# Residual and output bias of the last mixture folded into TensorE's PSUM accumulation

## The reference, cut to what matters

```
x = x + gnn0(layernorm(x), adj, ...)       # 4 heads, 2048 x 2048 mask
x = x + ffn0(layernorm(x), ...)            # 8 experts, top 2
x = x + gnn1(layernorm(x), adj, ...)       # one averaged attention
x = x + ffn1(layernorm(x), route_id, ...)  # the change touches this one
```

```
h = relu(flat @ Wi.T + bi)                          # 128 -> 256
for l in range(2):
    h = relu(h + shared_l(h) + routed_l(h))         # one expert per group of 32 rows
out = h @ Wo.T + bo                                 # 256 -> 128
x + out is returned
```

## Time and profile before

| what | value |
|---|---|
| time, median of 3 runs | 739.09 us (736.9 to 740.69) |
| the profiled execution's own time | 739.58 us |
| its span, first to last instruction | 737.8 us |
| PE busy, share of the span | 617.6 us, 84% |
| DVE busy | 526.4 us, 71% |
| ACT busy | 388.4 us, 53% |
| POOL busy | 164.8 us, 22% |
| chain that ended last | PE 65%, DVE 18%, ACT 7%, issue 5%, POOL 3%, DMA 1% |
| POOL L483, the adds of ysb to x | 16 instructions, 42.2 us, mean 2641 ns |
| ACT L1063, the evictions to ysb | 16 instructions of 277 to 278 ns |

### The profile page before, as it was taken

One profiled execution on the slowest core, in us unless ns is written; L12 is line 12 of the kernel. 1 busy time (PEld: TensorE's weight loads), 2 busy tenths in 40 slices (PEclk: granted clock), 3 DMA queues, 4 the chain that ended last, 5 costly groups with the idle time before them and its releaser, 6 DMA issues.

```text
span 737.8 us, 14828 instructions
## 1 busy us (share of the span) xinstructions
PE 617.6 (84%) x5288; PEld 467.8 (63%) x5288; DVE 526.4 (71%) x1071; ACT 388.4 (53%) x761; POOL 164.8 (22%) x130
## 2 busy tenths in 40 slices
PE   2856776999999999899999979984589889889696
PEld 1645664867868678677887636763547647647453
DVE  6699989677677776678663579269597998997300
ACT  1767895777867678567887455431022222222231
POOL 4201032011111111102111113416403603602100
PEclk9977995999999999999999989996769979969888
DMA  7446630011110111101111011010546716716643
GB/s 156 84 79 115 172 58 1 2 59 58 59 58 1 59 58 59 59 2 59 58 59 58 0 58 56 2 45 3 150 136 189 226 58 197 217 57 200 213 130 113
DMA packets 30702, 63.08 MB, mean 86 GB/s; under 512 B 4556, under 2 KB 7636, under 8 KB 30644
## 3 DMA queue, kind: packets, MB, share of 16 engines
q1 hardware_dynamic: 27156, 52.50, 23.5%
q0 software_dynamic: 2624, 9.44, 6.6%
q10 hardware_dynamic: 864, 0.33, 0.2%
HBM read 69.59 MB, written 1.05 MB: 96 GB/s over the span
## 4 chain that ended last, share of the span: by engine, by line
PE 65%; DVE 18%; ACT 7%; issue 5%; POOL 3%; DMA 1%; SPq 1%; DVEq 0%; ACTq 0%
PE bank L598 16%; PE bank L610 12%; PE bank L558 10%; PE bank L679 6%; PE bank L543 5%; PE bank L716 4%; PE bank L709 3%; ACT arena L956 2%; POOL reg_b L455 2%; DVE reg_c L1355 2%; DVE arena L1210 2%; PE bank L534 2%; DVE arena L1198 2%; ACT ysb L913 1%; PE bank L507 1%
## 5 line engine op out<-in xcount | busy, mean ns | idle before, releaser
L956 ACT ACTIVATE arena<-sbc,nd 128x512 bf16<-128x512 f32 x204 | 130.2, 718 | 33.5 <-PE bank L558 33.5
L448 POOL TENSOR_TENSOR x<-x,ysb 128x512 f32<-128x512 f32 x36 | 61.9, 1720 | 304.9 <-ACT ysb L913 300.6
L610 PEld LDWEIGHTS bank<-arena,reg_c 128*128 128x128 f32 x1024 | 116.8, 192 | 7.2 <-issue 7.2
L598 PE MATMUL bank<-hTc,arena 128*128 128x512 f32 x256 | 120.9, 628 | 0.0
L610 PE MATMUL bank<-arena,reg_c 128*128 128x128 f32 x1024 | 116.9, 275 | 0.0
L558 PE MATMUL bank<-reg_b,arena 128*128 128x99 bf16 x2048 | 102.4, 213 | 11.3 <-DVE arena L1210 11.2
L558 PEld LDWEIGHTS bank<-reg_b,arena 128*128 128x128 bf16 x2048 | 100.6, 101 | 14.1 <-issue 12.1
L903 ACT ACTIVATE reg_c<-bank,b 128x512 f32<-128x512 f32 x128 | 87.9, 688 | 36.3 <-PE bank L598 36.3
L1355 DVE SCALAR_TENSOR_TENSOR reg_c<-reg_b,nd,reg_c 128x512 f32<-128x512 f32 x144 | 96.3, 740 | 0.0
L1198 DVE TENSOR_TENSOR arena<-maskT,arena 128x2048 bf16<-128x2048 bf16 x48 | 60.8, 1266 | 49.8 <-ACT arena L956 49.6
L598 PEld LDWEIGHTS bank<-hTc,arena 128*128 128x128 f32 x256 | 51.1, 202 | 64.6 <-issue 64.6
(11 more groups left out here) (164 smaller groups left out, 729.1 us busy)
## 6 DMA issues: line engine op xcount, KB each, us to landing
arena<-in_wrT SPq DMA_DIRECT2D x128, 256.0 KB, 3.0
reg_c<-in_adj POOLq DMA_DIRECT2D x16, 512.0 KB, 5.9
arena<-in_w1T SPq DMA_DIRECT2D x16, 512.0 KB, 3.9
arena<-in_w2T SPq DMA_DIRECT2D x16, 512.0 KB, 4.8
x<-in_x SPq DMA_DIRECT2D x4, 256.0 KB, 4.6
out_x<-x POOLq DMA_DIRECT2D x4, 256.0 KB, 3.8
arena<-in_wsT SPq DMA_DIRECT2D x1, 512.0 KB, 3.7
arena<-in_gW ACTq DMA_DIRECT2D x2, 64.0 KB, 4.0
```

Source lines behind the costliest of these rows:

```text
L448: nc.gpsimd.tensor_tensor(xi, xi, ysb[:, e % 3, :].rearrange("p (t d) -> p t d", d=P), ALU.add).then_inc(s_acc, 1)
L598: mm(bank[b][:, :], w1[:, s, e % 2, c * P:(c + 1) * P], hTc[:, :], start=True, stop=True).then_inc(full[b], 1)
L610: last = mm(bank[b][:, i * P:(i + 1) * P], hid[:, e % 2, c, i * P:(i + 1) * P], w2[:, s, e % 2, c, :], start=(c == 0), stop=(c == HC - 1))
L956: last = af(ind[:, q, 1, j, :], sbc[:, h, :], ACT.Relu, bias=nd[:, q * QT + j, h:h + 1], scale=BIG)
```

## The change

POOL's bias add (L477) and its four adds a chunk (L483) are gone; POOL waits for the four evictions and stores. On PE `output` first multiplies the identity with the row tile of x, as moving operand, and a row of ones with the bias row `bo`, into the same 128 columns of PSUM, and then adds the two products as before. ACT copies the bank straight into x and no longer waits for a slot of `ysb`. Since x is addressed by the loop variable, `output` takes the chunk as a second argument.

```
@@ gpsimd
-                pool.wait_ge(s_xn, 3 * C + c + 1)
-                xi = x[:, c * CT:(c + 1) * CT, :]
-                nc.gpsimd.tensor_tensor(xi, xi, bo.unsqueeze(1).to_broadcast([P, CT, P]),
-                                        ALU.add).then_inc(s_xb, 1)
-                pool.wait_ge(s_xb, C + c + 1)
-                for i in range(CT):
-                    pool.wait_ge(ev["y"], FFN_Y + c * CT + i + 1)
-                    xi = x[:, c * CT + i, :]
-                    nc.gpsimd.tensor_tensor(xi, xi, ysb[:, 0, i * P:(i + 1) * P], ALU.add).then_inc(s_acc, 1)
-                pool.wait_ge(s_acc, FFN_Y + c * CT + CT)
+                pool.wait_ge(ev["y"], FFN_Y + c * CT + CT)
                 pool.dma_start(outv[:, c * CT:(c + 1) * CT, :],
                                x[:, c * CT:(c + 1) * CT, :]).then_inc(s_out, 16)
@@ tensor
-            def output(i):
+            def output(i, c):
                 r, b = i % 2, 3 + i % 2 * 2
                 ready(b - 1)
                 use(b, "y")
+                mm(bank[b][:, 0:P], ident[:, :], x[:, bass.ds(c * CT + i, 1), :].rearrange("p o d -> p (o d)"),
+                   start=True, stop=False)
+                mm(bank[b][:, 0:P], ones[0:1, :], bo[0:1, :], start=False, stop=False)
                 for kc in range(KC):
                     last = mm(bank[b][:, 0:P], htt[:, r, L, kc * P:(kc + 1) * P], woT[:, kc, :],
-                              start=(kc == 0), stop=(kc == KC - 1))
+                              start=False, stop=(kc == KC - 1))
                 last.then_inc(full[b], 1)
@@ scalar
-            def output(i):
+            def output(i, c):
                 b = 3 + i % 2 * 2
-                y_slot(CT)
+                k.event("y")
                 got(b)
-                af(ysb[:, 0, i * P:(i + 1) * P], bank[b][:, 0:P], ACT.Copy).then_inc(ev["y"], 1)
+                af(x[:, bass.ds(c * CT + i, 1), :].rearrange("p o d -> p (o d)"), bank[b][:, 0:P],
+                   ACT.Copy).then_inc(ev["y"], 1)
```

More of the change, by code:

```diff
@@ L773, in _, with chunk1 @@
             pe.wait_ge(s_wc, 1 + L * KC)
-            def chunk1(next_rows):
+            def chunk1(c, next_rows):
                 for t in range(QT):
@@ L794, in chunk1 @@
                         hidden(i + 1)
-                    output(i)
-            chunk1(2)
+                    output(i, c)
+            chunk1(0, 2)
             per = {"att": 2, "prob": 16, "rows": 4, "xn": 1, "hTc": 1, "ohx": 1, "htt": 20, "y": 4}
@@ L801, in _ @@
                 k.enter(c, 2, per)
-                chunk1((c + 1) % C)
+                chunk1(c - 1, (c + 1) % C)
                 k.leave(C - 2, per)
@@ L817, in _ @@
                 for j in pair:
-                    output(j)
+                    output(j, C - 1)
         @block.scalar
@@ L1081, in _ @@
                         hidden(i + 1)
-                    output(i)
+                    output(i, c - 1)
                 k.leave(C - 1, per)
```

## The result

| | kernel before | changed kernel |
|---|---|---|
| time, median of 20 runs each | 737.91 us (736.48 to 740.69) | 741.74 us (737.33 to 746.46) |
| ratio of the times | 1 | 1.0047, 95% interval 1.0028 to 1.0066 |
| profiled execution's own time, span | 739.58, 737.8 us | 742.76, 741.0 us |
| PE busy | 617.6 us x5288 | 623.0 us x5352 |
| POOL busy | 164.8 us | 117.2 us |

The ratio compares the means of the 20 runs: 3.5 us more, 0.47% of 738. Between the medians it is 3.8 us. Its interval leaves out 1, so the change is slower beyond the scatter of the runs, if only by a little. The forecast was +2.3 us against 739.09 us, the median of the three runs known then. The time, 741.7 us, lies within the range and 0.3 us from the forecast 741.4; that it is so close is in part luck, since those three runs lay 1.2 us above the median of 20.

A forecast was written before the change was run, and what follows sets the result against it. PE was taken to bound the dense stretches, DVE the pass starts. Added matmuls 4.11, address set up 0.48, bias add -2.49 and tail 0.2 summed to +2.3 us on 739.09: 741.4 us, range 737.8 to 744.3.

The forecast's parts named there:

- three signs of being wrong: Added instructions clearly above 0.457 us, first four L1355 staying at 3.56 us, or another clock course at the borders.
- The price of the added matmuls: PE, each output: four added instructions at 0.114 us, 0.457 us; three outputs a pass on the path, 4.11 us.
- Nothing is idle between: PE around one output: no idle time from ACT's last hidden tile to the following layer, so longer output moves everything.
- The address set up: PE behind the wait in loop passes: 0.08 us each, six on the path, +0.48 us.
- The fourth output and the border: End of a pass: PE's 2.97 us idle before xn covers this output's 0.46 us; uncovered, 1.4 us more in all.
- POOL's waiting adds cost DVE nothing: POOL's 128x128 adds: removing them frees 42.2 us of POOL time, and DVE gains nothing.
- The bias add: Start of each mixed pass: without POOL's 128x512 add, PE's wait ends 0.83 us earlier, 2.49 us over three.
- The rival that half of the gain is lost at the clock: Behind PE's wait: the 0.83 us won are spent at 1.2 GHz; sum +3.5 us, 742.6 us; chance 0.17.
- the clock stays up or rises earlier: Pass borders: more PE work, less idle time; saves up to 5.9 us in full, 735.5 us; chance 0.12.
- The tail: Last chunk: 0.91 us PE work, 0.15 hidden, 0.56 gained from POOL's add; +0.2 us, between 0.0 and 0.5.
- The slow rivals: Borders: POOL's store and cast hit layer norm harder, or bias add gives DVE no gain; each 743.9 us, chance 0.08.
- the clock rival: Pass borders: clock staying up or rising earlier, 1.96 us a pass; in two passes of three, the range's low end.

The follow-up runs named there:

- bias128: Changed kernel with the bias product taking the identity and 128 equal rows of bo, not one row; 736.53 us, ratio 0.9973 to the kernel before.
- the hoisted form: As bias128, with residual and bias products ahead of the wait for ACT's last hidden tile; 732.32 us, ratio 0.9904 to the kernel before.
- the second pair of executions: Kernel before and changed kernel, both unchanged, profiled once more; wait's end to first turn summed to 20.51 us and 18.33 us.
- 64 rows: Changed kernel with 64 rows of ones and of bo in place of one; one execution, 1.38 us from output to next layer.
- the constant address: Changed kernel with the residual reading row tile i of chunk 0 in every chunk; one execution, dense stretches 33.64, 33.64, 33.65 us.

## Why the prediction came out right, point by point

**What bounds.** Right. PE pays in the dense stretches, DVE at a pass's start: each removed or added piece came out where the windows had put it. The prediction named three signs of being wrong, and two of them are in the trace: the added instructions took clearly more than 0.457 us, and the clock at the borders took another course. The total is right, the sum behind it only in part.

**The price of the added matmuls.** Mis-sized. The forecast took 4 x 0.114 = 0.457 us from a run of equal shapes; measured are 0.83 us an output. The step that failed was to charge the one-row product by L574 beside L573: their durations (272 and 277 ns) are equal, but a duration does not contain the distance to the neighbour. The starts of the two would have warned of it in the trace of before. These lines are from the routing products of the last chunk of the first mixture, where 128 rows and one row alternate:

```profile
404.40 0.39 PE L573 MATMUL bank<-wgT,hTc 128*128 128x8 f32 x2
404.72 0.38 PE L574 MATMUL bank<-bg,ones 1*128 1x8 f32 x2
405.03 1.60 PE L598 MATMUL bank<-hTc,arena 128*128 128x512 f32 x2
```

The starts are 0.32 and 0.31 us apart at the full clock although the products have only 8 columns; in bias128 a product of 128 columns between others of 128 rows came in 0.22 us.

**What of it lay on the path.** Part of the dear price was covered by a wait I had overlooked. The dense stretch of the first pass grew by 2.09 us, 0.70 us an output and not 0.83. These are ACT and PE of the kernel before behind the output of the earlier trace rows:

```profile
564.81 0.63 ACT L1045 ACTIVATE sbc<-bank,arena 128x128 f32<-128x128 f32 x2
565.49 1.13 PE L709 MATMUL bank<-arena,sbc 128*128 128x256 f32 x4
566.56 1.09 PE L716 MATMUL bank<-arena,sbc 128*32 128x256 f32 x16
```

L709 starts just when ACT's next tile is written, 0.14 us behind L706, and L716 comes 1.07 us later. In the changed kernel ACT is done long before, L700 follows L697 in 0.11 us, and L707 follows at 555.22, 0.96 us later. That gives 0.03 + 0.11 = 0.14 us back (0.14 - 0.11 and 1.07 - 0.96), and 0.83 - 0.14 = 0.69 us are left. "Nothing is idle between" was thus wrong in the small: right behind `output` PE had a second wait, with the dearer restart that follows one. This is also why the hoisted form cost less than I expected: there PE goes from the start of `hidden` to L700 in 1.45 us, before in 1.32 us, and gets 0.11 us back behind it.

**The address set up.** Right in kind, 0.10 us each instead of 0.08 us.

**The fourth output and the border.** Right: +0.03 us over three borders, the cover of 2.97 us held. The store did not come earlier against the layer norm, as I had it: at the second border it starts 1.25 us after the first step, before 0.82 us. Two steps are stretched there as before.

**POOL's waiting adds cost DVE nothing.** Right; the twelve tiles take 8.03 us with and without them.

**The bias add.** Right to 0.01 us for the wait itself, 2.50 against 2.49 us, and right that DVE does not stand for the whole of POOL's 1.52 us: the one stretched instruction loses 0.84 us, and 0.44 us of POOL's 1.52 are its own loss (1.08 us alone).

**The clock.** The rival that half of the gain is lost at the clock had its sign wrong. That it gives +3.5 us, what was measured, is chance. From the wait's end to the first turn PE needed 1.6 us less over three passes, 2.2 us less in the second pair of executions, and 1.2 us less in the kernel without the add. In eleven profiled executions of kernels without the add at that place the sum was 15.96 to 21.38 us, ten of them below 19.6; with it twice 20.5. The granted clock of the changed kernel reached 1.00 at about 544 us, 11.5 us after the transposes; in the kernel before at about 549 us, 15 us after them. The prediction had "the clock stays up or rises earlier" as another rival, for another reason (more work for PE), with 5.9 us in full; something of this kind happened, to 1.6 us.

How far it belongs to the change shows in the runs. The granted clock of the whole program was 0.909 on the mean in the 23 runs of the kernel before, 0.913 in the 12 without the add, and 0.919 in the 20 of the changed kernel. From the first transposes on it was 0.87 in both traces of the kernel before and 0.90 to 0.93 in the eleven others. The clock also goes with the spread of the changed kernel's own runs: its fastest, 737.33 us, had 0.932, its slowest, 746.46 us, 0.916. That kernels without the add at the border run at the higher clock is thus shown; what makes it rise is not. In the trace with 64 rows, PE's first wait ended as early as in the changed kernel and the clock still rose 14.8 us after the transposes.

**The tail.** Mis-sized: +1.70 us in place of +0.2 us. 0.92 us of it is the last two outputs up to the store. The forecast had 0.91 - 0.15 us for PE there and -0.56 us for POOL; measured are +1.45 and -0.53 us, so it is the price of the products again. 0.27 us is the way up to the first turn (9.39 us after the transposes, before 9.12), over a stretch that was 8.4 to 9.8 us in all the traces. The other 0.51 us lie between the first turn and the end of PE's wait for the last expert weights (15.21 us, before 14.70). That the first two outputs vanish in this wait was right: up to the next turn, which follows it, the kernels with 64 rows and with the constant address, which have all the added products, need 15.64 and 15.56 us, the kernel before 15.68 and 15.49 us. Why the changed kernel needs 16.19 and 16.14 us stays open.

**The slow rivals** did not happen: the layer norm's border stayed the same, and DVE's gain was real. The low end of the range is worked out wrongly: two passes of three at the clock rival are 741.4 - 3.9 = 737.5 us, not 737.8.

So the total came near because costs that were 2.3 us (dense stretches) and 1.5 us (tail) too small met a gain of 1.6 us that I had not counted; that leaves +4.5 us in the traces, and +3.5 us in the means of 20 runs. The stages and waits were right; what failed is the price of the added products in the dense stretches and the tail, 0.83 us in place of 0.457 us at an output, and the clock, which the sum had at nothing. That the misses went against each other is luck.

## What to carry to other kernels

Price an added matmul by the distance between starts in the very neighbourhood it will have, weight rows included; here a one-row product for a bias between products of 128 rows cost 1.38 - 0.77 = 0.61 us, where one of 128 rows, with the identity and a replicated bias, cost 1.00 - 0.77 = 0.23 us. Put products that need nothing new ahead of the wait and not behind it: the same two products, with 128 rows, cost 0.31 to 0.42 us an output behind the wait and 0.02 us ahead of it. And ask first whether the add had to move at all: POOL's bias add, only issued later, gave 3.8 us (0.5%) in the passes and the last chunk with one edited line.

## What the runs showed of the hardware

A change of the number of weight rows between neighbouring float32 matmuls cost 0.19 us at each change, with one row and with 64 rows alike, and of two equal one-row products in a row the second cost 0.23 us. At such a change the weight load and the matmul start together, where otherwise the load is 0.11 us ahead; the same is seen where the weights go from 32 to 128 columns. The first product behind a wait at which PE stood costs 0.11 us more than one in a run; a wait that was over before costs nothing (L730 in the hoisted kernel follows in 0.22 us).

A DVE instruction of 128x512 took 1.58 us in place of 0.74 beside POOL's 128x512 add, and the add 1.52 us in place of 1.08. POOL's store and its cast each stretched one of DVE's shortest steps from 0.16 to 0.58 us. POOL's waiting adds of 128x128, up to 15.7 us long, cost DVE nothing.
